# The first two layers of four batches as one stream of stages in place of a loop over pairs

## The reference

```python
h = layernorm(x) * (1 + ca) + sa
x = x + ga * attention(h)
h = layernorm(x) * (1 + cb) + sb
x = x + gb * second(h)
```

## Time and profile before

| what | us |
|---|---|
| median of 3 runs | 2548.73 |
| lowest and highest | 2548.28, 2555.42 |
| the profiled execution | 2561.89 |
| its span, first to last instruction | 2559.7 |
| TensorE busy | 2134.3 (83%) |
| VectorE busy | 1833.0 (72%) |
| GpSimd busy | 1546.3 (60%) |
| ScalarE busy | 1472.3 (58%) |

### The profile page before, as it was taken

One profiled execution on the slowest core, in us unless ns is written; L12 is line 12 of the kernel. 1 busy time (PEld: TensorE's weight loads), 2 busy tenths in 40 slices (PEclk: granted clock), 3 DMA queues, 4 the chain that ended last, 5 costly groups with the idle time before them and its releaser, 6 DMA issues.

```text
span 2559.7 us, 87557 instructions
## 1 busy us (share of the span) xinstructions
PE 2134.3 (83%) x34508; PEld 1517.4 (59%) x34508; DVE 1833.0 (72%) x3805; ACT 1472.3 (58%) x2864; POOL 1546.3 (60%) x797
## 2 busy tenths in 40 slices
PE   3788857889748888888988988898888989889886
PEld 2664445654526666666656666666666666666664
DVE  3784466754658878787778777777877877778783
ACT  1782345743536666666666566665666666665662
POOL 0110001100069888887888878888888878878780
PEclk9998877999779999999999999999999999999998
DMA  4000000000112222222222222222222222222221
GB/s 93 2 2 1 0 6 1 2 1 1 34 30 67 58 66 77 74 58 64 52 76 73 60 66 75 73 59 55 61 77 74 58 62 54 75 74 60 66 50 34
DMA packets 94715, 126.26 MB, mean 49 GB/s; under 512 B 27484, under 2 KB 42466, under 8 KB 94306
## 3 DMA queue, kind: packets, MB, share of 16 engines
q1 hardware_dynamic: 94306, 120.54, 18.6%
HBM read 21.91 MB, written 1.05 MB: 9 GB/s over the span
## 4 chain that ended last, share of the span: by engine, by line
PE 45%; issue 27%; DVE 14%; ACT 8%; POOL 4%; SPq 1%; DVEq 1%; ACTq 0%; DMA 0%; POOLq 0%
PE oo L548 11%; PE pj L548 10%; PE tr L551 9%; PE sc L548 9%; ACT arena L1534 6%; PE tr L548 4%; DVE arena L1360 2%; DVE arena L1366 2%; DVE arena L1358 2%; DVE xn L1066 1%; POOL arena L1873 1%; DVE arena L1380 1%; DVE arena L1382 1%; POOL arena L1871 1%; DVE arena L1391 1%
## 5 line engine op out<-in xcount | busy, mean ns | idle before, releaser
L1871 POOL TENSOR_TENSOR arena<-arena 128x1024 f32<-128x1024 f32 x192 | 455.4, 2372 | 213.8 <-DVE arena L1360 202.8
L551 PE MATMUL tr<-ident,arena 128*128 128x128 f32 x3004 | 454.8, 289 | 134.2 <-ACT arena L1534 79.6
L1873 POOL TENSOR_TENSOR arena<-arena,half_neg 128x16 f32<-128x16 f32 x192 | 564.0, 2938 | 0.0
L1534 ACT ACTIVATE arena<-pj 128x512 f32<-128x512 f32 x576 | 334.5, 593 | 380.8 <-PE pj L548 369.7
L1534 ACT ACTIVATE arena<-tr 128x512 f32<-128x512 f32 (+2 forms) x880 | 461.4, 569 | 156.7 <-PE tr L551 129.7
L551 PEld LDWEIGHTS tr<-ident,arena 128*128 128x128 f32 x3004 | 358.8, 147 | 227.7 <-ACT arena L1534 96.7
L1358 DVE TENSOR_TENSOR arena<-pj,rtab 128x512 f32<-128x512 f32 x384 | 263.1, 685 | 274.5 <-ACT arena L1534 255.4
L1879 POOL TENSOR_TENSOR arena<-arena 128x1024 f32<-128x1024 f32 x192 | 365.4, 1903 | 24.6
L1534 ACT ACTIVATE arena<-arena 128x1024 f32<-128x1024 f32 (+4 forms) x424 | 281.8, 668 | 111.5 <-DVE arena L1382 49.5
L1837 POOL TENSOR_TENSOR rstd<-rstd,half_neg 128x4 f32<-128x4 f32 x40 | 40.9, 1022 | 499.0 <-DVE rstd L1061 499.0
L1360 DVE TENSOR_TENSOR arena<-pj,rtab 128x512 f32<-128x512 f32 x384 | 261.6, 681 | 0.0
(11 more groups left out here) (250 smaller groups left out, 3847.8 us busy)
## 6 DMA issues: line engine op xcount, KB each, us to landing
slab<-arena SPq DMA_DIRECT2D x576, 128.0 KB, 2.4
slab<-arena SPq DMA_DIRECT2D x336, 64.0 KB, 2.1
wqkv<-in_L_ffn_Wqkv SPq DMA_DIRECT2D x18, 512.0 KB, 3.6
wo<-in_L_ffn_Wo SPq DMA_DIRECT2D x6, 512.0 KB, 4.6
w<-in_L_ffn_W SPq DMA_DIRECT2D x6, 341.0 KB
arena<-in_L_attn_x SPq DMA_DIRECT2D x4, 256.0 KB, 2.9
arena<-in_L_ffn_W SPq DMA_DIRECT2D x1, 1024.0 KB
out_x<-arena SPq DMA_DIRECT2D x4, 256.0 KB, 2.3
```

Of the source, the lines that this page charges most:

```text
L551: return nc.tensor.transpose(o, i, ident[0:i.shape[0], 0:i.shape[0]])
L1534: return nc.scalar.activation(o, i, f, **k)
L1871: p_.tensor_tensor(r_, r_, rb[:, k, :], ALU.add).then_inc(sum_ok, 1)
L1873: p_.tensor_tensor(rr[:, k, :], rr[:, k, :], half_neg[:, 0:HL], ALU.pow).then_inc(pow_ok, 1)
```

## The change

The loop over pairs goes. All four batches pass through layer 0's attention as one stream of 64 heads, then through one of 32 experts, then through 16 heads of layer 1, which come in two blocks of 8. `NORMS` gives the norms one order for all engines. x of every batch is loaded straight into the space of its `H`, before anything else needs it, and the modulation columns are read from `modT` itself. In the stream of heads `r` is the head within the batch: the next batch's norm A, stacks and values stand beside batch b's heads (now with a second bank, oo, for one stack of two at r = 4, and for the values at 12), and the batch before has its output and norm B there; the router of batch 0 stands at r = 12 to 15 of the last batch. Beside the experts (`beside`) stand the last batch's output, the other routers, norm C of three batches, memory of batches 0 and 1 and layer 1's stacks of batch 0. hes and hsc, which were in the arena, now share the space of `Qst` and `Kst`. In the setup 12 loads are counted by `ld_const`, 11 by a new `ld_mid`; the zeroing of VH stands ahead of the loads, and norm A of batch 0 runs from its own rows without being turned first. The copy of x into XT at the end of a pair goes, as x lives in XT now. The windowed layers are not touched.

```diff
-FILL = 4
...
+FILL = {3: (0,), 4: (1, 2), 7: (3,), 12: (4,), 13: (5,), 14: (6,), 15: (7,)}
...
+NORMS = [("A", 0), ("A", 1), ("A", 2), ("B", 0), ("A", 3), ("B", 1), ("B", 2), ("B", 3),
+         ("C", 0), ("C", 1), ("C", 2), ("C", 3), ("D", 0), ("D", 1), ("D", 2), ("D", 3)]
...
-        sp.dma_start(dst, src, allow_slow_non_contiguous=True).then_inc((ld_const, ld_late)[late], 16)
+        sp.dma_start(dst, src, allow_slow_non_contiguous=True).then_inc((ld_const, ld_mid, ld_late)[late], 16)
...
+    load_x(0)
...
+    for b in range(1, B):
+        load_x(b)
...
-    with sp.Fori(2, B) as b:
-        load_x(b)
...
+    def first_layer(h):
+        b, r = divmod(h, H0)
+        if b >= B:
+            return
+        if b < B - 1:
+            if r == 0:
+                pe.wait_ge(st_lo, made(0, b + 1))
+                x_turn(b + 1, AUX)
+            if r == 2:
+                pe.wait_ge(x_in, b + 2)
+                ln_back_("A", b + 1)
+            if r == 3:
+                normed("A", b + 1)
+            if r == 7 and b >= 1:
+                pe.wait_ge(x_add, b)
+            if r == 12 and b >= 1:
+                normed("B", b - 1)
+            for f, i in enumerate(FILL.get(r, ())):
+                if f == 0:
+                    pe.wait_ge(st_lo, made(0, b + 1) + i)
+                else:
+                    wait(pe, o_tok, h // 4 - 1)
+                stack(0, b + 1, i, oo[:, 0] if f else AUX)
+            if r == 12:
+                pe.wait_ge(o_tok, h // 4 - 1)
+                value_rows(0, b + 1, oo[:, 0])
+        if b >= 1:
+            if r == 5:
+                if b < B - 1:
+                    pe.wait_ge(st_lo, made(0, b + 1) + 3)
+                out_turn(0, b - 1, AUX)
+            if r == 6:
+                out_project(0, b - 1, AUX)
+            if r == 8:
+                if b < B - 1:
+                    pe.wait_ge(st_lo, made(0, b + 1) + 4)
+                pe.wait_ge(x_add, b)
+                ln_in_("B", b - 1)
+            if r == 11:
+                ln_back_("B", b - 1)
+        if b == B - 1 and r == 12:
+            normed("B", B - 2)
+            pe.wait_ge(ld_late, n_late)
+            logits(0, AUX)
...
+    def logits(b, bank):
         for t in range(T):
-            last = mm(tr[:, 0, t * NE:(t + 1) * NE], h_[:, t * P:(t + 1) * P], wg[:, :])
+            last = mm(bank[:, t * NE:(t + 1) * NE], H(b)[:, t * P:(t + 1) * P], wg[:, :])
         last.then_inc(lg_mm, 1)
...
+    def beside(b, n):
+        if n == 0:
+            pe.wait_ge(routed, b + 1)
...
-        up(0)
-        pe.wait_ge(routed, b + 1)
-        for t in range(T):
-            last = tp(sc[0:NE, 0, t * P:(t + 1) * P], rt[:, 11, t * NE:(t + 1) * NE])
-        last.then_inc(s_tr, 1)
-        spread(0)
-        pe.wait_ge(s_ev, b + 1)
-        mm(oo[:, 0], mb2[:, :], sT[0:NE, :], stop=False)
-        for e in range(1, NE):
-            if e == 2:
-                pe.wait_ge(x_add, p * 6 + 2 + u_)
-                ln_in_(li)
-            if e == 4:
-                ln_back_(p, li)
-            up(e)
-            spread(e)
-            down(e - 1)
-        down(NE - 1)
-        pe.wait_ge(ln_out, p * 6 + li + 1)
-        pe.wait_ge(x_add, p * 6 + 3 + u_)
-    pe.sem_inc(x_tr, 1)
-    with pe.Fori(0, B // 2) as p:
...
-        pe.wait_ge(x_in, p * 2 + 2)
-        ln_in_(0)
-        ln_back_(p, 0)
-        attention(p, 0)
-        pe.wait_ge(ld_late, n_late)
-        experts(p, 0)
-        experts(p, 1)
-        attention(p, 1)
-        pe.wait_ge(y_in, p * 2 + 3)
+                last = tp(sc[0:NE, 0, t * P:(t + 1) * P], GATES[b % 2][:, t * NE:(t + 1) * NE])
+            last.then_inc(s_tr, 1)
+        if b == 0:
+            if n == 1:
+                group_out(0, B * H0 // 4 - 1)
+            if n == 2:
+                out_turn(0, B - 1, AUX)
+            if n == 3:
+                out_project(0, B - 1, AUX)
+        if n == 2 and b < B - 1:
+            normed("B", b + 1)
+            pe.wait_ge(s_ev, b + 1)
+            logits(b + 1, sc[:, 0])
+        if b >= 2:
+            if n == 1:
+                normed("C", b - 2)
+                mem_query(b - 2, sc[:, 1])
+            if n == 3:
+                memory(b - 2, (sc[:, 1], oo[:, 1]))
+        m = ("B", B - 1) if b == 0 else ("C", b - 1)
+        if n == 4:
+            pe.wait_ge(x_add, B + b)
+            if b >= 2:
+                pe.wait_ge(am_ok, b - 1)
+            ln_in_(*m)
+        if n == 6:
+            ln_back_(*m)
+        if b == B - 1 and n >= 1:
+            if n == 1:
+                pe.wait_ge(s_ev, B)
+            pe.wait_ge(st_lo, made(1, 0) + n - 1)
+            stack(1, 0, n - 1, sc[:, 0])
+            if n == NE - 1:
+                value_rows(1, 0, sc[:, 1])
+    def experts():
+        for j in range(NE * B):
+            b, n = divmod(j, NE)
+            if j >= 1:
+                beside(b, n)
+                up(j)
+            spread(j)
+            if j >= 1:
+                down(j - 1)
+        down(NE * B - 1)
+    def into_experts(h):
+        first_layer(h)
+        if h == B * H0:
+            pe.wait_ge(biased, B * H0 * T)
+            up(0)
+        if h == B * H0 + 1:
+            beside(0, 0)
...
+    def second_layer():
+        pe.wait_ge(st_lo, made(1, 0) + 7)
+        stack(1, 0, 7, sc[:, 0])
+        normed("C", 1)
+        stack_banks(1, 1, 0, 4)
+        pe.wait_ge(x_add, 2 * B)
+        ln_in_("C", 3)
+        stack_banks(1, 1, 4, 8)
+        pe.wait_ge(st_lo, made(1, 1))
+        value_rows(1, 1, sc[:, 0])
+        ln_back_("C", 3)
+        pe.wait_ge(v_ev, B + 2)
+        heads(1, 0, 8, lambda h: None)
+        normed("C", 3)
+        mem_query(2, sc[:, 1])
+        stack_banks(1, 2, 0, 4)
+        group_out(1, 1)
+        stack_banks(1, 2, 4, 8)
+        out_turn(1, 0, AUX)
+        value_rows(1, 2, sc[:, 0])
+        out_project(1, 0, AUX)
+        pe.wait_ge(v_ev, B + 3)
+        pe.wait_ge(qk_ev, 3)
+        memory(2, (sc[:, 0], sc[:, 1]))
+        out_turn(1, 1, oo[:, 0])
+        pe.wait_ge(am_ok, 3)
+        mem_query(3, sc[:, 1])
+        pe.wait_ge(st_lo, made(1, 3))
+        stack_banks(1, 3, 0, 4)
+        out_project(1, 1, oo[:, 0])
+        stack_banks(1, 3, 4, 8)
+        pe.wait_ge(x_add, 2 * B + 1)
+        ln_in_("D", 0)
+        value_rows(1, 3, sc[:, 0])
+        pe.wait_ge(v_ev, B + 4)
+        pe.wait_ge(qk_ev, 4)
+        memory(3, (sc[:, 0], sc[:, 1]))
+        pe.wait_ge(am_ok, 4)
...
+        heads(1, 8, 16, ending)
+        group_out(1, 3)
+        out_turn(1, 3, tr[:, 0])
+        pe.wait_ge(x_add, 2 * B + 3)
+        pe.wait_ge(o_tok, B * H0 // 4 + 4)
+        ln_in_("D", 2)
+        out_project(1, 3, pj[:, 0])
+        ln_back_("D", 2)
+        pe.wait_ge(x_add, 2 * B + 4)
+        ln_in_("D", 3)
+        pe.wait_ge(y_in, 4)
+        ln_back_("D", 3)
+    normed("A", 0)
+    stack_banks(0, 0, 0, 4)
+    pe.wait_ge(x_in, 1)
+    value_rows(0, 0, sc[:, 0])
+    stack_banks(0, 0, 4, 8)
+    heads(0, 0, B * H0, into_experts)
+    experts()
+    second_layer()
+    pe.wait_ge(y_in, B + 1)
...
-    ve.wait_ge(ld_const, n_const)
+    for u_ in range(2):
+        v.memset(VH[u_][:, :, 0:H0, :], 0.0)
+    v.memset(wst[:, :, :, :, 3 * GW:P], 0.0)
+    ln_first("A", 0)
...
+    ln_second("A", 0)
+    ve.wait_ge(x_tr, 1)
+    v.tensor_copy(X(0), sc[:, 1]).then_inc(x_in, 1)
+    ve.wait_ge(ld_mid, n_mid)
...
+    def first_before(h):
+        b, r = divmod(h, H0)
+        if b < B - 1 and r == 0:
+            ln_first("A", b + 1)
+        if b < B - 1 and r == 2:
+            ln_second("A", b + 1)
+        if 1 <= b < B and r == 11:
+            ln_second("B", b - 1)
+    def first_layer(h):
+        b, r = divmod(h, H0)
+        if b >= B:
+            return
+        if b < B - 1:
+            if r == 0:
+                ve.wait_ge(x_tr, b + 2)
+                v.tensor_copy(X(b + 1), AUX).then_inc(x_in, 1)
+            for f, i in enumerate(FILL.get(r, ())):
+                low(0, b + 1, i, oo[:, 0] if f else AUX)
+            if r == 12:
+                value_rows(0, b + 1, oo[:, 0])
+        if b >= 1:
+            if r == 6:
+                add_out(0, b - 1, AUX)
+            if r == 8:
+                ln_first("B", b - 1)
+        if b == B - 1:
+            if r == 12:
+                route_in(0, AUX)
+            if r == 13:
+                route_sum(0)
+                route_pick(0, 0)
+            if r == 14:
+                route_pick(0, 1)
+            if r == 15:
+                route_out(0)
...
+    def experts():
+        for j in range(NE * B):
+            b, n = divmod(j, NE)
+            m = ("B", B - 1) if b == 0 else ("C", b - 1)
+            if n == 0:
+                ve.wait_ge(s_tr, b + 1)
+                v.tensor_copy(sT[0:NE, :], sc[0:NE, 0, :]).then_inc(s_ev, 1)
+            if n == 4:
+                ln_first(*m)
+            ve.wait_ge(m_relu, j * 2 + 2)
+            ve.wait_ge(m_bc, j + 1)
+            if j >= 2:
```

(90 more changed lines are left out.)

831 lines of the change are left out of this document (403 added, 428 removed).

## The result

The changed kernel takes 2464.4 us (median of 4 runs, 2463.7 to 2467.5) where the kernel before took 2552.1 on the same chip (2548.3 to 2560.2): a ratio of 0.966, 95% interval 0.963 to 0.968. The forecast was 2436. So the gain is 88 us and not 113, and the time lies just above the stated range of 2412 to 2464. Every run here counts as undisturbed, so all of them can be compared.

A forecast was written before the change was run, and what follows sets the result against it. Seams where one chain goes engine by engine were the target. Setup 22.5, stacks 12.9, heads 289.7, handover 1.5, experts 155.7, then 13, 65.1, 30 and tail 18 sum to 608.4, 113.1 under 721.5; 2548.7 becomes 2436 us, range 2412 to 2464.

The forecast's parts named there:

- the six layers behind them (1838.2 us) start from the last `y_in` and don't change: Six windowed layers after the first two: stay at 1838.2 us, so only the first two layers' 721.5 us can move.
- I take the same microseconds off: From profiled time to median: the median was 13.2 us under the profiled 2561.9; 113.1 off 2548.7 gives 2436.
- Heads: Layer 0's stream of 64 heads: 289.7 us, including added heads, fills, outputs, copies of x, seams and the first router.
- the first batch's fill: Next batch's stacks, values and first norm beside batch 0's heads: 12.7 us a fill, bounds 8 to 16.
- Experts: Stage of 32 experts: 155.7 us, of which 31 experts at 3.87 us, 23.2 for side work and 12.5 for waits.
- The waits at batch 3's stacks: Beside batch 3's experts, each stack waits at TensorE for VectorE's low half before it: 10.4 us together.
- The clock: TensorE's clock through the experts: granted 1.00, the fall going with the router gaps; remaining seams keep their low level.
- (a): Whole kernel: the time as summed, 2436 us, own range 2418 to 2455; chance 0.70.
- (b): Expert stage held by side work: 24 steps each wait 1.2 us more on VectorE, 30 more, 2466 us; chance 0.13.
- (c): Side work nearly free: fills of 8 us, no waits beside the experts, 27 less, 2409 us; chance 0.14.
- (d): Stream of 64 heads falls to 1.2 GHz: 152 us more, kernel slower at 2588 us; chance 0.02.
- (e): A wait undoes the whole gain, such as fills holding heads for their batch's drain: within 0.3%; chance 0.01.

The follow-up runs named there:

- covered192: Changed kernel with 192 bare signals on TensorE, spread over five stretches (64, 14, 26, 28, 60) where it was expected to wait: 2452.2 us.
- before_shift54: Kernel before with 54 more bare signals on TensorE ahead of its first wait: 2576.9 against 2555.4 us, ratio 1.0088.
- covered192_moved: Changed kernel with 192 bare signals on TensorE, 28 moved behind the last norm's transposes, others shifted: 2446.6 us against 2469.1 of the changed kernel.
- experts_clear: Changed kernel with layer 1's first-batch stacks moved from beside the fourth batch's experts to behind the last expert: 2465.6 us against 2469.1.

## Why the prediction was wrong, point by point

**The step that failed: "the six layers behind them (1838.2 us) start from the last `y_in` and don't change. So the change can only move the 721.5".** They took 1853.0. Shown: the length of these layers goes with the place of TensorE's loop in the blocks of its instruction queue. 54 instructions put the kernel before where the changed one is and lengthen them by 18.1; 192 put the changed one near where the kernel before is and shorten them by 19 (1852.9 to 1834.0). In medians of all runs on one chip it is 21.5 and 22.5 us. That the time goes through the fetching of instructions is argued, not shown. The waits for issue fit it between places 196 and 206 on one side and 4 on the other (35.4 and 34.9 against 49.1 and 48.0, 13 to 14 of the 18 to 19 us; covered192 has 40.3) and don't fit it at 228, where they are 32.8 and the layers are long all the same. TensorE's busy time for the same 30812 matmuls moves too: 1582.0 to 1583.5 us in the three runs at 196, 1594.0 at 206 and 1592.1 to 1602.1 at all other places, with a granted clock of 0.97 at 196 and of 0.96 or 0.97 elsewhere. So a part may go through the clock; no run parts the two. Why places from 196 to 206 are good, 164 half so and 228 not, and what the places of the other engines' loops do, stays open.

**How much of the miss this is, and a term that did not hold: "I take the same microseconds off".** In medians the miss of 28 has two parts. The kernel before took 2552.1 beside the changed one and not 2548.7, which is 3.3. And the gain was 87.7 and not 113.1, which is 25.4; of these the place is worth 21.5 by before_shift54 (22.5 by covered192_moved). The 3 to 4 that are left fit the first two layers: before_shift54 ends them at 718.0, with the same work as in the kernel before and its signals covered, where the prediction's trace has 721.5. From 718.0 to 609.2 is 108.8, 4.3 short of the 113.1.

By the profiled executions alone the shares look otherwise: 2561.9 - 113.1 = 2448.8, then 14.8 for the six layers and 0.8 for the first two give 2464.4, and the 13.2 that were taken off to come to the median make up the rest. The changed kernel's profiled execution, 2464.4, is at its median, so there was nothing to take off. The profiled execution of the kernel before was a long one; that some of its 13.2 lies in the 1838.2, whose usual length would then be near 1832 (2552.1, less 2.2 outside the span, less 718.0), is an estimate. Other sets of runs of the kernel before have medians of 2555.4, 2561.7 and 2562.4, so chip and day move it as well.

**First two layers: 609.2 for 608.4, right in sum, and with errors that cancel.** Setup 21.2 (22.5): the twelve loads landed at 10.18 (11). Stacks 12.6 (12.9), last head to experts 1.3 (1.5), seam behind the experts 12.8 (13), between the blocks 34.8 (30), two times eight heads 65.3 (65.1), tail 20.0 (18).

Heads 280.2 for 289.7. The mis-sized term is the first batch's fill: to head 16's mask the forecast has the 66.8 of the kernel before (125.66 - 58.9) with a copy and a seam, 68.9, and the changed kernel takes 59.9 (93.70 - 33.8). From head 2 to head 16 it takes 57.2, where before it was 62.98, so that fill cost 6.9 at the forecast's pace and not 12.7, below its bound of 8. Its stacks and norms stand beside other heads now; which of that makes it cheaper was not tried, and the overlooked signals are worth about 2 us over all 64 heads. The middle batches took 73.8 and 72.8 for 74.1 (16 paces, a fill, an output, a copy and a seam), the last 15 heads 58.8 for 60.8 (15 paces, an output, the router). From the last mask to the end of the stage, where the first expert's products now lie, it is 14.9, where before it was 11.8.

Experts 161.0 for 155.7: side work and waits were 41.0 and not 35.7. The waits at batch 3's stacks are the ones named. Its stacks, values and waits, priced at 7 x 0.86 + 0.9 + 10.4 = 17.3, cost 13.8 by the run experts_clear, 1.7 of them through the clock; some of the waits (for memory and norm) stay in that run. So the 5.3 too little lie elsewhere in the stage, and no run parts them.

**The clock** went nearly as forecast: 0.99 granted through the experts, where the earlier trace rows has 0.91 and 1.00 was forecast, with the one fall in batch 3 shown above. Low levels are left in the second eight heads of layer 1 (0.82) and in the tail (0.67).

**Rivals.** (a)'s sum of the first two layers held, in part by luck, since the 9.5 too much in the heads is cancelled by 5.3 too little in the experts and 4.8 between the blocks; its own range of 2418 to 2455 was too low by 9. (b) was forecast at 2466, near the time, but for another reason: of its 30 us more in the experts 5 came. (c) came true in the first batch's fill alone; (d) and (e) did not occur. The prediction did name "a changed length of the six layers" as what would prove it wrong, but gave it no price.

## What to carry to other kernels

A stretch of code that is not edited can still change its time, where it is a long loop of matmuls and the edit ahead of it adds or drops instructions: here by up to 24 us, 1% of the kernel. So compare the unedited stretch first, and before a small gain or loss is put down to an edit, run it with several numbers of empty instructions in spots where the engine waits; one number can miss the effect (64 and 128 changed nothing here, 54 and 192 did). Take medians beside each other on one chip: one profiled execution can be 13 us off. And work put beside a busy engine is not free: the stacks cost about as much beside the experts (12.1 us, 13.8 with a fall of the clock) as behind them (11.6).

## What was not expected of the hardware

The place of the loop moves the six layers between 1832.7 and 1856.8 us, and not in a smooth way: 1847.5 at 164, 1834.0 at 196, 1856.5 at 228. The Trainium skill (Runtime: NRT & Kernel Launch, Instruction fetch mechanics) has blocks of 16 KiB, 256 instructions, fetched while the one before runs, with the crossing mostly hidden; the size agrees with the 16.4 KB a packet here, but TensorE has 33 to 55 us of waits for issue in six layers of 42 blocks each. That these waits are crossings is not shown. The same section says that a taken branch to a block that isn't held forces a fetch; the trace agrees, with a wait of TensorE at each new round of the loop (timeline of the changed kernel, first and second of four):

```profile
1177.46 0.50 PE L564 MATMUL pj<-wq_hi,xs_hi 128*128 128x512 f32 x1 [2.42 <-issue]
...
1478.00 0.79 PE L564 MATMUL pj<-wq_hi,xs_hi 128*128 128x512 f32 x1 [2.39 <-issue]
```

Every place has this wait, 2.4 to 2.8 us in the mean of the four at places 3, 4, 132, 164, 196 and 206, and 3.5 at 68 and 3.2 at 228. So it is mainly a cost of the loop; of what sets the places apart it is some 4 us at most.

A bare signal on TensorE took 0.15 us ((619.8 - 610.1) / 64 between the runs with 128 and 64), so that 192 of them at the start, with some 10 us of waiting over them, cost the 20 us that they win.
